# Selective scan: the product of u and B computed on VectorE, one iteration ahead of its scan, instead of on GpSimd

## The reference, cut to what matters

```
x = x + scan(layernorm(x))
def scan(x, W_xproj, b_xproj, W_dt, b_dt, A_log):
    proj = x @ W_xproj.T + b_xproj
    dt_r, Bm, Cm = split(proj, [128, 128 + 16])
    dt  = softplus(dt_r @ W_dt.T + b_dt)          # batch, length, 256
    A   = -exp(A_log)                             # 256 x 16
    dA  = exp(dt * A)                             # batch, length, 256, 16
    dBX = dt * Bm * x                             # batch, length, 256, 16
    h[l] = dA[l] * h[l-1] + dBX[l]                # along the length, per channel and state
    y   = sum over the 16 states of h * Cm
```

## Time and profile before

| | |
|---|---|
| median of three runs | 1311.08 us |
| profiled execution: time / span of its instructions | 1314.02 us / 1312.2 us |
| mean granted clock of TensorE | 0.922 of full |
| busy TensorE / VectorE / ScalarE / GpSimd | 85% / 67% / 50% / 50% |
| scan loop, first to last scan start | 354.32 to 490.70 us |
| in the loop's lines: scans busy / products on GpSimd busy | 102.8 us x32 / 106.0 us x32 |
| idle of VectorE just before scans | 35.9 us |

### The profile page before, as it was taken

How to read it: one execution, slowest core, us unless ns; L and a number is a source line. 1 busy time by engine, 2 the same in 40 slices (tenths; PEclk the granted TensorE clock), 3 DMA queues, 4 the chain that set the end, 5 groups by cost and what they waited for, 6 DMA issues and landing times. The chain is left out here.

```text
span 1312.2 us, 22467 instructions
## 1 busy us (share of the span) xinstructions
PE 1115.9 (85%) x6776; PEld 926.3 (71%) x6776; DVE 875.2 (67%) x2076; ACT 651.2 (50%) x2059; POOL 655.3 (50%) x649
## 2 busy tenths in 40 slices
PE   5499978797276774799989989999997999999998
PEld 4366645585144442688878988898887888888887
DVE  5676684734677777577877787777877455555555
ACT  4266643221467763366556655665555344333333
POOL 3623260453377774365546545654452455555554
PEclk9699988597689886899999999999998799999999
DMA  7000000001011212000200200000001111111111
GB/s 223 0 1 0 0 0 10 1 0 52 36 53 65 71 66 68 16 1 2 73 2 1 74 2 2 1 1 1 1 1 27 36 48 45 40 47 48 48 48 44
DMA packets 43957, 41.28 MB, mean 31 GB/s; under 512 B 6160, under 2 KB 39984, under 8 KB 43872
## 3 DMA queue, kind: packets, MB, share of 16 engines
q1 hardware_dynamic: 42144, 39.02, 9.7%
q10 hardware_dynamic: 1728, 1.18, 0.3%
HBM read 39.08 MB, written 1.11 MB: 31 GB/s over the span
## 5 line engine op out<-in xcount | busy, mean ns | idle before, releaser
L1700 POOL TENSOR_TENSOR hid_l<-hid,hid_h 128x512 fp32r<-128x512 f32 x66 | 85.7, 1298 | 132.5 <-ACT hid_h L1669 132.5
L1326 POOL TENSOR_TENSOR qr<-r_part_a,r_part_b 128x512 f32<-128x512 f32 x64 | 82.4, 1287 | 129.5 <-DVE r_part_b L1360 128.4
L1340 POOL TENSOR_TENSOR prob<-prob,rden 128x128 f32<-128x128 f32 (+1 forms) x256 | 124.4, 509 | 37.5 <-DVE rden L1411 37.5
L1750 DVE TENSOR_TENSOR hid<-psum,silu 128x512 f32<-128x512 f32 x66 | 45.6, 691 | 130.8 <-ACT silu L1667 130.8
L899 POOL TENSOR_TENSOR drive<-u,b_all 128x1024 f32<-128x1024 f32 x32 | 106.0, 3331 | 53.6 <-DVE h L998 33.4
L998 DVE TENSOR_TENSOR_SCAN h<-decay,drive 128x1024 f32<-128x1024 f32 x32 | 102.8, 3249 | 35.9 <-POOL drive L899 22.4
L1286 ACT ACTIVATE prob<-psum,neg_max 128x128 f32<-128x128 f32 (+1 forms) x256 | 106.0, 424 | 37.2 <-DVE neg_max L1400 36.8
L1742 DVE SCALAR_TENSOR_TENSOR x<-psum,weight,x 128x256 f32<-128x256 f32 x264 | 108.8, 475 | 0.0
L73 PE MATMUL psum<-xt_h,gu_l 128*128 128x512 f32 x264 | 106.1, 402 | 2.4 <-POOL gu_l L1685 2.4
L75 PE MATMUL psum<-xt_h,gu_h 128*128 128x512 f32 x264 | 104.9, 397 | 0.0
L74 PE MATMUL psum<-xt_l,gu_h 128*128 128x512 f32 x264 | 104.7, 396 | 0.0
(11 more groups left out here) (250 smaller groups left out, 3796.0 us busy)
## 6 DMA issues: line engine op xcount, KB each, us to landing
b_all<-scan_b_rows SPq DMA_DIRECT2D x16, 512.0 KB, 3.6
early<-in_L_ffn_Wq_dram SPq DMA_DIRECT2D x4, 1024.0 KB, 5.3
early<-in_L_ffn_Wo_dram SPq DMA_DIRECT2D x4, 1024.0 KB, 7.7
raw<-in_L_ffn_Wg_dram SPq DMA_DIRECT2D x32, 128.0 KB, 2.2
raw<-in_L_ffn_Wu_dram SPq DMA_DIRECT2D x32, 128.0 KB, 2.3
raw<-in_L_ffn_Wd_dram SPq DMA_DIRECT2D x32, 128.0 KB, 2.2
x<-_attn_hidden_states_dram SPq DMA_DIRECT2D x8, 128.0 KB, 4.7
early<-in_L_ffn_w_up_q_dram SPq DMA_DIRECT2D x1, 1024.0 KB, 6.4
```

What stands on the lines that cost most here:

```text
L1326: pool.tensor_tensor(qr[:, i, :], part_a[:, slot, :], part_b[:, slot, :], ALU.add).then_inc(roped, 1)
L1340: ins = pool.tensor_tensor(at, at, rden[:, s % 2, i:i + 1].to_broadcast([P, (i + 1) * P]), ALU.mult)
L1700: pool.tensor_tensor(hid_l[:, j, cols], hid[:, c, :], f(hid_h[:, j, cols]), ALU.subtract)\
```

## The change

The GpSimd stream ends after its work on `dtr`. The product of each step is issued on VectorE with the same operands, the same waits and the same semaphore. `drives(0)` comes ahead of the loop, and in step `at` the product of step at + 1 is issued before the scan of step `at`.

```diff
@@ block.gpsimd
-                for at in range(STEPS):
-                    n, k = at // KD, at % KD
-                    if n == 0:
-                        pool.wait_ge(dt_ready, k + 1)
-                    else:
-                        pool.wait_ge(scanned, at - KD + 1)
-                    pool.wait_ge(b_loaded[n % BBUF], 16 * (n // BBUF + 1))
-                    pool.tensor_tensor(drive[:, k, :], u[:, k, :], b_all[:, n % BBUF, :], ALU.mult).then_inc(driven, 1)
@@ block.vector
+                def drives(at):
+                    n, k = at // KD, at % KD
+                    if n == 0:
+                        dve.wait_ge(dt_ready, k + 1)
+                    else:
+                        dve.wait_ge(scanned, at - KD + 1)
+                    dve.wait_ge(b_loaded[n % BBUF], 16 * (n // BBUF + 1))
+                    dve.tensor_tensor(drive[:, k, :], u[:, k, :], b_all[:, n % BBUF, :], ALU.mult).then_inc(driven, 1)
+
+                drives(0)
                 for at in range(STEPS):
                     n, k = at // KD, at % KD
+                    if at + 1 < STEPS:
+                        drives(at + 1)
                     dve.wait_ge(decay_ready, at + 1)
                     dve.wait_ge(driven, at + 1)
                     if n >= 1:
```

## The result

Four runs of the changed kernel have a median of 1278.3 us (1277.89 to 1278.9); the kernel before, measured beside it, 1311.35 us. The ratio is 0.974, with a 95% interval of 0.9715 to 0.9765: faster, by 33 us. Forecast were 1280 us and 31 us less. The profiled execution took 1278.64 us, its span is 1276.7 us.

A forecast was written before the change was run, and what follows sets the result against it. The prediction took the loop to be bound by one resource VectorE and GpSimd use in turn. 30.7 - 0.24 + 1.2 = 31.7 us, rounded to 31, gave 1311.08 - 31 = 1280 us, range 1275 to 1296.

The forecast's parts named there:

- The bound: Scan loop: a VectorE scan and a GpSimd product never progress at once; four pieces of 2.20 fill 8.79 us, two steps.
- The step: One loop step on VectorE after the change: scan 2.28 + 0.03 + product 1.23 - 0.09 = 3.45 us, within 3.42 and 3.60.
- The first scan: Loop start: drives(0) and drives(1) come before the first scan, which starts 0.24 us later.
- From first to last scan start: Whole scan loop: 30 x 3.45 + 2.18 = 105.7 us against 136.38, so 30.7 less.
- The tail: From the last scan's end to the stage's end: 7.0 us at full clock instead of 8.17, 1.2 less.
- stayed slow: Rival, 5%: TensorE's clock never rises in the loop, its 5.2 us a step sets the pace; +25 us, 1336 us.
- swung: Rival, 13%: TensorE at 1.2 GHz half of the time, 3.9 us a step, scans wait for turns; gain 16 us, 1295 us.
- idle each step: TensorE in the loop after the change: 3.45 - 2.65 = 0.8 us of idle every step, clock expected to stay at 2.4 GHz.
- The start: Loop start: TensorE begins at the lower clock, two turns and an add take 1.97 + 1.97 + 3.62 us, mostly within ScalarE's slack.
- The steps of ScalarE: Decay to decay with a weigh between and no idle: 3.17 us, under VectorE's 3.45 by 0.28.
- the two rivals of the clock: TensorE's clock in the loop: swinging (13%, 1295 us) or staying slow (5%, 1336 us).

The follow-up runs named there:

- additional product: Changed kernel plus one GpSimd product per step (two SBUF inputs, 128x1024) into a tile nobody reads; 1342.9 us, median of 2.
- additional copy: Changed kernel plus one GpSimd copy per step (one SBUF input, 128x1024) into a tile nobody reads; 1304.89 us, median of 8.
- half move: Against the kernel before, only the products of channel group 0 go to VectorE, those of group 1 stay on GpSimd; 1287.02 us, ratio 0.9821.
- changed, again: The changed kernel, unaltered, run again on the same chip as the two-buffer version; 1281.93 us, median of 5.
- not ahead: Changed kernel with each VectorE product issued just ahead of its own step's scan, not one step earlier; 1279.5 us, median of 4.
- two buffers: Changed kernel with a second pair of buffers for drive, so a product waits for a scan four steps back; 1273.67 us, ratio 0.971.
- two buffers, again: Changed kernel with a second pair of buffers for drive, run once more beside the unaltered changed kernel; 1274.7 us, median of 5.
- the memset: Changed kernel plus one GpSimd memset per step (128x2048, writes SBUF, reads nothing) into a tile nobody reads; 1279.66 us, median of 2.
- the run without products: Changed kernel without the products of all states but the first, output wrong; 1269.87 us, median of 2.

## Why the prediction was right, point by point

**The bound.** "One resource that VectorE and GpSimd use in turn" was read from the order of time and holds: additional product, additional copy and half move all show it. What the resource is, no run shows; the prediction needed only that it is used in turn.

**The terms.** The step was to be 3.45 us and is 3.46, start to start 2.32 for the scan and 1.14 for the product. The first scan was to come 0.24 us later: from line 988 or 980 to the first scan it is 354.32 - 347.49 = 6.83 before and 353.40 - 346.33 = 7.07 after, 0.24 more. From first to last scan start was to be 105.7 us and is 106.0, 30.4 less. The tail from the last scan's end, 457.19 + 4.46 = 461.65, to 468.80 is 7.15 us against 8.17, 1.0 less instead of 1.2. Sum 31.2 us, forecast 31.7, rounded to 31. The terms came out one by one, so the hit is not owed to errors that cancel.

**The rest of the 33.** The profiled executions differ by 35.4 us, 4.2 more than the stage explains. Of these 1.16 lie ahead of the stage and 3.0 in the attention stage behind it. The other kernels suggest that this is spread: up to the first `dt` (line 988 before, 980 after) all run the same instructions, yet over the twelve profiled executions it starts anywhere from 344.0 to 350.6 us. The first scan differs more, since the kernels put none, one or two VectorE products ahead of it, and the additional product on GpSimd holds it up.

| profiled kernel | first `dt` | first scan | first to last scan | attention stage | from its end |
|---|---|---|---|---|---|
| before | 347.5 | 354.3 | 136.4 | 499.5 | 308.1 |
| changed | 346.3 | 353.4 | 106.0 | 496.5 | 308.0 |
| changed, again | 348.2 | 355.3 | 106.0 | 496.7 | 308.0 |
| not ahead | 345.9 | 352.0 | 108.4 | 495.6 | 307.8 |
| half move | 344.0 | 350.1 | 118.8 | 494.8 | 305.7 |
| additional product | 349.9 | 359.1 | 170.6 | 494.5 | 308.0 |
| two buffers | 345.2 | 352.3 | 101.7 | 496.9 | 307.9 |
| two buffers, again | 350.6 | 357.6 | 101.7 | 494.0 | 308.0 |

(us; the attention stage goes from the last start of its norm, line 112, to the first start of the next norm, the last column from there to the end of the span.) On the second chip visit the changed kernel's median was 1281.93 beside 1311.46, 29.5 us less. The two comparisons, 33.1 and 29.5, lie on both sides of the 31.2 of this stage. What makes the stages ahead differ by up to 6.6 us from one execution to the next was not tried.

**The rivals.** TensorE neither stayed slow nor swung: after the first windows the granted clock is 1.00, with 0.65 us of idle each step (forecast 0.8). The start was as feared, two turns and one add at 1.2 GHz, and ScalarE's slack took it: no scan waited. That small idles can make the clock swing, as the Trainium skill, "TensorE: Matmul & The Clock Gate", section "A second HAM failure mode: psum-queue depth-cycling", has it, doesn't happen at this size of idle here. The forecast of 0.8 had counted the 2.65 us between two turns that follow at once; with a wait it is 406.98 - 404.17 = 2.81 us from a turn's start to the add's end. The steps of ScalarE were put at 3.17 us and measured 3.10 once it was the limit. The times of the two rivals of the clock, 1295 and 1336 us, were not put to a test.

The rule of the Trainium skill named with the memset ("SBUF — State Buffer", section "SBUF: two separate sides"), by which a VectorE operation with two SBUF inputs collides only with a GpSimd operation that reads SBUF, agrees with all three additional operations: the memset added 0.00 us a step, the copy 0.84, the product 2.15.

## What to carry to other kernels

Where operations of VectorE and GpSimd come in two lengths, check whether the long one ends one pure duration after the end of the other engine's operation. If so, the two may be taking turns, as here, and an additional operation that nobody waits for can test it. Where they do, the sum of pure durations is the limit, whatever the busy shares say. Move such work to where its pure duration is shorter (here 1.14 us against 2.2), even onto the busier engine, and before that ask what the other engines' steps are, since they cap the gain (ScalarE at 3.10 of 3.46 us). Work left to GpSimd beside two-input operations of VectorE did no harm here where it only wrote SBUF; where it read SBUF, it did.

## What the runs showed of the hardware that was not expected

- The order of asking fits every collision shown: in the run with the additional product, GpSimd's request at 400.75 went ahead of the scan recorded from 401.85. In the half move the second scan had started at 403.49, GpSimd's product is recorded from 403.65 and ran only after it, but ahead of VectorE's product recorded from 405.78.
- A wait on the operation just ahead on VectorE costs 0.12 us against a close follower where that is a scan (in the medians of the loop, a start 0.04 us after the recorded end instead of 0.08 before it), 0.17 where it is a product (0.09 after instead of 0.08 before). Without it the scan takes 2.20 us from start to start instead of 2.32, and the product 1.12 instead of 1.14, for which no run shows a cause; together this gave the 4.3 us.
- Recorded durations on ScalarE grow where it is the limit: in the run without products the record of a decay climbs from 1.15 us at the start of the loop to 2.27 and stays there (1.79 in the mean), and weigh's single copies are recorded as 1.02 us in the mean instead of 0.40, while the start-to-start spacing of the steps is 3.10 us. There the spacing is the time and the mean isn't. Why the records grow was not tried.
